# Cross-attention with a gate on one core: running maximum and shift on pairs of score tiles

## The reference

```
memory_proj    = einsum('bme,de->bmd', memory, W_mem)
scores         = einsum('bnd,bmd->bnm', x, memory_proj) / sqrt(512)
attn           = softmax(scores, axis=-1)
memory_context = einsum('bnm,bmd->bnd', attn, memory_proj)
gate  = sigmoid(einsum('bnf,df->bnd', concat[x, memory_context], W_gate) + b_gate)
fused = x + gate * memory_context
out   = fused * rsqrt(mean(fused**2, axis=-1) + 1e-6) * norm_w
```

## Time and profile before

| | us |
|---|---|
| median of 3 runs (lowest, highest) | 561.93 (561.55, 562.57) |
| the profiled execution | 561.31 |
| its span in the trace | 559.5 |
| PE busy | 538.0 |
| DVE busy | 503.5 |
| ACT busy | 335.7 |
| POOL busy | 134.0 |
| one batch of the loop (from 296.17 to 362.19) | 66.02 |

### The profile page before, as it was taken

The page is one execution under the profiler, slowest core; times in us unless marked ns, Lnnn a source line. Parts: engine busy times, 40 slices in busy tenths (PEclk is TensorE's granted clock), DMA queues, the critical chain, the costliest instruction groups (busy, mean ns, idle before and its releaser), DMA issues.

```text
span 559.5 us, 8972 instructions
## 1 busy us (share of the span) xinstructions
PE 538.0 (96%) x2416; PEld 436.4 (78%) x2416; DVE 503.5 (90%) x847; ACT 335.7 (60%) x633; POOL 134.0 (24%) x102
## 2 busy tenths in 40 slices
PE   6999999999999999999999999999999999999992
PEld 5877888878888788878888788887888778887881
DVE  3789859999899998899988998999988999889976
ACT  4666636665567655586366764766556754657534
POOL 0005500244002530055101550024400351005600
PEclk9999999999999999999999999999999999999997
DMA  9974362511684107821276115752078311210033
GB/s 224 261 130 68 95 107 77 100 63 34 141 174 107 37 23 154 170 75 37 89 142 135 56 37 123 164 100 73 0 159 178 85 37 69 69 38 21 0 115 112
DMA packets 184338, 54.25 MB, mean 97 GB/s; under 512 B 161528, under 2 KB 174848, under 8 KB 184320
## 3 DMA queue, kind: packets, MB, share of 16 engines
q1 hardware_dynamic: 183792, 53.52, 41.2%
q10 hardware_dynamic: 528, 0.52, 0.3%
HBM read 45.63 MB, written 8.39 MB: 97 GB/s over the span
## 4 chain that ended last, share of the span: by engine, by line
PE 65%; DVE 19%; issue 10%; ACT 2%; SPq 2%; DMA 1%; ACTq 0%; DVEq 0%
PE bank L355 14%; PE bank L357 13%; PE bank L356 13%; PE bank L516 7%; PE bank L517 7%; PE bank L518 7%; DVE p_lo L830 6%; DVE s L871 3%; DVE fused L976 2%; DVE fused L983 2%; DVE gate L897 2%; ACT fused L688 2%; DVE gate L926 2%; SPq L239 2%; DMA x_raw<-in_x_dram 1%
## 5 line engine op out<-in xcount | busy, mean ns | idle before, releaser
L1147 POOL TENSOR_TENSOR psum_rows<-psum_rows,p_tmp 128x512 f32<-128x512 f32 (+1 forms) x88 | 122.4, 1391 | 86.5 <-ACT p_tmp L665 85.4
L830 DVE TENSOR_TENSOR p_lo<-p_tmp,p_hi 128x512 fp32r<-128x512 f32 (+1 forms) x104 | 92.2, 888 | 4.8 <-ACT p_hi L627 4.8
L665 ACT ACTIVATE p_tmp<-s 128x512 f32<-128x512 f32 (+1 forms) x104 | 65.2, 627 | 45.1 <-DVE s L871 44.4
L1147 POOL TENSOR_TENSOR psum_rows<-p_tmp 128x512 f32<-128x512 f32 x8 | 10.8, 1352 | 309.0 <-ACT p_tmp L665 309.0
L355 PE MATMUL bank<-q_hi,mt_hi 128*128 128x512 f32 (+1 forms) x208 | 81.8, 393 | 0.0
L516 PE MATMUL bank<-p_hi,mem_hi 128*128 128x512 f32 (+1 forms) x208 | 81.2, 390 | 0.1
L356 PE MATMUL bank<-q_lo,mt_hi 128*128 128x512 f32 (+1 forms) x208 | 81.2, 390 | 0.0
L357 PE MATMUL bank<-q_hi,mt_lo 128*128 128x512 f32 (+1 forms) x208 | 81.2, 390 | 0.0
L517 PE MATMUL bank<-p_lo,mem_hi 128*128 128x512 f32 (+1 forms) x208 | 81.1, 390 | 0.0
L518 PE MATMUL bank<-p_hi,mem_lo 128*128 128x512 f32 (+1 forms) x208 | 81.0, 389 | 0.0
L627 ACT ACTIVATE s<-bank 128x512 f32<-128x512 f32 (+1 forms) x104 | 62.0, 596 | 19.4 <-PE bank L357 18.9
(11 more groups left out here) (91 smaller groups left out, 1028.4 us busy)
## 6 DMA issues: line engine op xcount, KB each, us to landing
mem_raw<-in_ctx_dram SPq DMA_DIRECT2D x48, 256.0 KB, 3.0
mem_blocks<-in_ctx_dram SPq DMA_DIRECT2D x64, 136.0 KB
x_again<-in_x_dram SPq DMA_DIRECT2D x32, 256.0 KB, 2.7
out_dram<-fused SPq DMA_DIRECT2D x32, 256.0 KB, 2.1
x_raw<-in_x_dram SPq DMA_DIRECT2D x112, 64.0 KB, 2.1
mem_blocks<-in_ctx_dram SPq DMA_DIRECT2D x56, 64.0 KB, 2.0
x_raw<-in_x_dram SPq DMA_DIRECT2D x4, 256.0 KB, 4.8
gate<-in_L_xattn_W_gate_dram SPq DMA_DIRECT2D x2, 512.0 KB, 5.7
```

The source lines that it names most:

```text
L665: nc.scalar.activation(p_tmp[0:r, t % TMP_RING, :], s[0:r, t, :], ACT.Exp, scale=float(D) ** -0.5).then_inc(exp_done, 1)
L830: return nc.vector.tensor_tensor(dst, src, hi.bitcast(F32), ALU.subtract)
L1147: nc.gpsimd.tensor_tensor(psum_rows[0:r, :], a, p_tmp[0:r, t % TMP_RING, :], ALU.add).then_inc(p_added, 1)
```

## The change

The running maximum and the shift work on two score tiles at a time, 1024 columns in one operation.

- `run` holds two tiles. `running_max(b, p)` takes the pair p (1 to 5) and starts when both tiles of the pair are copied. `fold_max` then takes the maximum of the two halves, and `last_max` takes in tile 12, of 65 rows. That is 7 operations instead of 12.
- `shift(b, p)` subtracts the spread maximum from a pair, with the bank read twice through a broadcast pattern. Tile 12 stays alone. That is 7 operations instead of 13. Two pairs are shifted ahead of the loop over the tiles (before: three tiles), and within it the pair t/2 + 2 at each even t up to 8 (before: tile t + 3 at each t up to 9).
- In the scoring stage the pair's maximum stands behind the low part and the block transpose of its step, and `last_max` stands behind all low parts of the memory. Before, tile 12 was taken in ahead of the low parts 4 and 5.
- The waits on `run_done` and `shifted` count by pairs.

```diff
-            def running_max(b, t):
+            def running_max(b, p):
-                dve.wait_ge(s_copied, MT * b + t + 1)
-                r = rows(t)
-                if t == 1:
-                    a = s[0:r, 0, :]
-                else:
-                    a = run[0:r, :]
-                    dve.wait_ge(run_done, (MT - 1) * b + t - 1)
-                nc.vector.tensor_tensor(run[0:r, :], a, s[0:r, t, :], ALU.max).then_inc(run_done, 1)
+                dve.wait_ge(s_copied, MT * b + 2 * p + 2)
+                if p == 1:
+                    a = s[:, 0:2, :]
+                else:
+                    a = run[:, :, :]
+                    dve.wait_ge(run_done, MP * b + p - 1)
+                nc.vector.tensor_tensor(run[:, :, :], a, s[:, 2 * p : 2 * p + 2, :], ALU.max).then_inc(run_done, 1)
+            def fold_max(b):
+                dve.wait_ge(run_done, MP * b + MP - 2)
+                nc.vector.tensor_tensor(run[:, 0, :], run[:, 0, :], run[:, 1, :], ALU.max).then_inc(run_done, 1)
+            def last_max(b):
+                dve.wait_ge(run_done, MP * b + MP - 1)
+                dve.wait_ge(s_copied, MT * (b + 1))
+                nc.vector.tensor_tensor(run[0:LAST, 0, :], run[0:LAST, 0, :], s[0:LAST, MT - 1, :],
+                                        ALU.max).then_inc(run_done, 1)
...
+                if p < MP - 1:
+                    ts = slice(2 * p, 2 * p + 2)
+                    nc.vector.tensor_tensor(s[:, ts, :], s[:, ts, :],
+                                            bank[MAX_BANK][:, :].rearrange("p (a n) -> p a n", a=1).broadcast_to([P, 2, N]),
+                                            ALU.subtract).then_inc(shifted, 1)
...
             def softmax(b, t, with_x):
-                if t + 3 < MT:
-                    shift(b, t + 3)
+                if t % 2 == 0 and t // 2 + 2 < MP:
+                    shift(b, t // 2 + 2)
...
                 transpose_mem(b, 2)
                 for p in range(MP):
-                    if p >= 1:
-                        running_max(b, 2 * p)
                     if p + 2 < MP:
                         mt_lo_part(b, p + 2)
                     if p + 3 < MP:
                         transpose_mem(b, p + 3)
-                    if 2 * p + 1 < MT:
-                        running_max(b, 2 * p + 1)
+                    if 1 <= p < MP - 1:
+                        running_max(b, p)
+                    if p == MP - 2:
+                        fold_max(b)
                     for q in SPLIT_BY_SCORES.get(p, []):
                         mem_lo_part(b, q)
+                last_max(b)
```

More of the change, by code:

```diff
@@ L113, in xattn_kernel @@
         norm_rows = sb("norm_rows", [P, D])
-        run = sb("run", [P, N])
+        run = sb("run", [P, 2, N])
         psum_rows = sb("psum_rows", [P, N])
@@ L417, in transpose_max @@
             def transpose_max(b):
-                pe.wait_ge(run_done, (MT - 1) * (b + 1))
+                pe.wait_ge(run_done, MP * (b + 1))
                 pe.wait_ge(s_copied, MT * (b + 1))
@@ L424, in transpose_max @@
                     last = nc.tensor.transpose(
-                        bank[S_BANK][:, j * P : (j + 1) * P], run[:, j * P : (j + 1) * P], ident[:, :])
+                        bank[S_BANK][:, j * P : (j + 1) * P], run[:, 0, j * P : (j + 1) * P], ident[:, :])
                 last.then_inc(pe_max_t, 1)
@@ L447, in row_sums @@
                 else:
-                    pe.wait_ge(shifted, MT * (b + 1))
+                    pe.wait_ge(shifted, MP * (b + 1))
                 for j in range(NT):
@@ L654, in exp @@
             def exp(b, t, first):
-                act.wait_ge(shifted, MT * b + t + 1)
+                act.wait_ge(shifted, MP * b + t // 2 + 1)
                 if t >= TMP_RING:
@@ L864, in reduce_max, with shift @@
                                         AX.X, ALU.max).then_inc(col_max_done, 1)
-            def shift(b, t):
-                if t == 0:
+            def shift(b, p):
+                if p == 0:
                     dve.wait_ge(pe_max_rows, b + 1)
-                r = rows(t)
-                nc.vector.tensor_tensor(s[0:r, t, :], s[0:r, t, :], bank[MAX_BANK][0:r, :],
-                                        ALU.subtract).then_inc(shifted, 1)
+                if p < MP - 1:
[4 more added lines that the diff above has]
+                else:
+                    nc.vector.tensor_tensor(s[0:LAST, MT - 1, :], s[0:LAST, MT - 1, :], bank[MAX_BANK][0:LAST, :],
+                                            ALU.subtract).then_inc(shifted, 1)
             def p_lo_part(b, t):
@@ L1046, in iteration @@
                     shift(b, 1)
-                    shift(b, 2)
                     for t in range(MT):
```

## The result

| | before | after |
|---|---|---|
| median of the runs, us | 561.93 (561.55 to 562.57) | 574.89 (574.29 to 575.68) |
| the profiled execution, us | 561.31 | 574.29 |
| its span, us | 559.5 | 572.5 |
| PE busy, us | 538.0 | 537.0 |
| DVE busy, us | 503.5 | 492.8 |

A forecast was written before the change was run, and what follows sets the result against it. PE was taken as the bound, busy 65.15 of 66.02 us per batch. The terms 1.6 - 0.25 + 6 x 1.65 + 1.65 - 0.3 = 12.6 us move the median from 561.93 to 574.5 us; range 568 to 579.5.

The forecast's parts named there:

- The bound: Loop batch: PE busy 65.15 of 66.02 us; less DVE time gives back at most about 1 us per batch.
- The price of a pair: DVE operations on two tiles: engine held 1.13 us, result after 1.21 us; bounds 1.06 and 1.20 us.
- The maximum: End of scoring: last_max starts at 299.13, transposes at 299.88, so PE loses 1.60 us per batch.
- The shifts and add_bias: Shift to weighted 0: add_bias 0 later, one larger wait replaces two at gate_x; weighted 0 late by 1.68 us.
- rival (a): Low part of tile 2 starts before POOL's fourth addition: weighted 0 late by 1.3, not 1.65 us; 572.1 us; 20%.
- The sum: Whole kernel: first batch, six loop batches at 1.65 us and last batch give 12.6 us more, median 574.5.
- (b): First shift depends less on context 0, delay half absorbed at gate_x: 0.85 us lost per batch, 568.7 us; 10%.
- (c): Longer DVE operations let POOL in once more ahead of add_bias 0: about 1 us per batch, 581 us; 10%.
- (d): DVE decides: maximum not late on PE, 0.8 us per batch off the waits at gate_x, 556.3 us; 4%.
- DVE's slack: Past tile 4: DVE has 1.1 us less to do than PE's delay, so xt, q, mt and u come early enough.

The follow-up runs named there:

- e9: Kernel before with the shift on pairs, the maximum on single tiles, and add_bias 0 to 3 moved to t = 2, 3, 5, 6: 551.20 us.
- e12: Kernel before with POOL adding only 64 of the 512 columns: 550.34 us.
- e1: Changed kernel with last_max (tile 12) directly behind the fold, ahead of low parts 3, 4 and 5 of the memory: 577.67 us.
- e6: Changed kernel with the pair shifts in the loop at odd t instead of even t, so six tiles are shifted ahead of add_bias 0: 571.79 us.
- e7: Changed kernel with tiles 0 to 9 as four maximum pairs, tiles 10 to 12 single, pairs shifted at t = 1, 4, 6, 8, 10: 573.56 us.
- e5: Changed kernel with POOL adding only 64 of the 512 columns: 564.45 us.
- e3: Changed kernel with the shift back on single tiles, so only the maximum is on pairs: 575.31 us.
- e8: Kernel before, all on single tiles, with the shifts of tiles 6 to 12 one step later: 563.61 us.
- e10: Kernel before, all on single tiles, with add_bias 0 to 3 moved to t = 2, 3, 5, 6: 564.48 us.
- e11: Four maximum pairs with early fold, tiles 10 to 12 single, pair shifts at even t, add_bias at t = 2, 3, 5, 6; against kernel before: 554.07 us.

## Why the prediction was right

**The bound.** PE was read as the bound, with 0.87 us of idle time per batch. It held: DVE was busy for 10.7 us less and the kernel gained nothing by it. What better timing on DVE can give back was put too low, at about 1 us per batch: e9 and e12 give back 1.5 (66.02 to 64.5), because a stop costs PE its idle time and a slow restart.

**The price of a pair.** Taken as 1.13 us to the next start and 1.21 us in length; the two groups measured 1.208 us (shift) and 1.212 us (maximum):

```profile
L883 DVE TENSOR_TENSOR s<-s,bank 128x1024 f32<-128x1024 f32 x48 | 57.2, 1208 | 0.0
L841 DVE TENSOR_TENSOR run<-run,s 128x1024 f32<-128x1024 f32 x32 | 38.8, 1212 | 7.7 <-ACT s L627 7.7
```

The broadcast bank costs nothing extra. Two shifts in a row take 2.34 us, so the next start comes after 1.13 us, and the fixed part of an operation that reads a bank is 0.07 us (2 x 0.60 less 1.13). The Trainium skill (VectorE: DVE Perf Modes, the section on the TRN2 errata) gives 120 cycles for a PSUM source, which by the prediction's estimate is 0.125 us; here the measurement decides.

**The maximum.** Predicted: last_max from 299.13, transposes from 299.88, late by 1.60 us. Measured in the same frame (minus 6.55): 299.18 and 300.00, late by 1.72 us, of which 1.48 are seen as idle. Of the missing 0.12 us, 0.05 is the later start of last_max, and 0.07 the way from DVE to PE, 0.13 us here and not the 0.06 us taken from add_bias.

**The shifts and add_bias.** gate_input 3 was put at 311.95 and stood at 312.12; the terms given for it (311.35 + 1.6 + 0.5 - 1.4) add up to 312.05, so 0.1 us of the miss is a slip in the sum. From it, POOL's fourth addition was put at +2.70 us and came at +2.70, the low part of tile 2 at +2.85 and came at +2.84, add_bias 0 at +4.5 and came at +4.47. The thin margin of rival (a), 0.15 us, fell as forecast, to POOL, by 0.14 us; that is right but partly luck, since other times of the stepping are off by as much. gate_x 3 no longer waits, and weighted 0 starts at 322.89 in this frame (329.44), 1.77 us late where 1.68 were forecast.

**The sum.** Forecast 12.6 us, measured 12.96 (574.89 - 561.93). By parts, from the starts of the transposes in batches 1 and 7: up to batch 1 forecast 2.95, measured 3.14 (100.24 to 103.38), the excess being in the first transposes, which were 1.85 us late (38.01 to 39.86) and not 1.6; six batches of the loop forecast 9.9, measured 10.1 (396.14 to 406.24); the rest forecast -0.25, measured -0.3 (from 63.14 to 62.87 us).

**What the prediction had not seen.** It presented the 1.60 us as the price of the maximum alone. e1 shows that it is the larger of two lags at the end of scoring: with the order of the last maximum put right, DVE is still behind with the pair, the fold and the low parts, and PE waits for add_bias 0 instead. It also read DVE's slack as safe up to the end of the batch; that held for the change, but e6 and e7, which shift later, used it up at mt_lo. The rivals (b), (c) and (d) did not occur; the waits that (b) relied on were POOL's, as e5 and e12 show.

## What to carry to other kernels

Merging operations saves a fixed part each, but makes the first result of the merged work later and lets it start only when the last of its inputs is there; where the merged work ends a stage that another engine waits for, take the last pieces one by one, and put nothing ahead of them that this engine does not need. Follow the engine that had its order changed to the end of the period, and not just to the next wait. Where a two-operand operation can be held by another engine's access, place the results that the bounding engine waits for ahead of the operations that are held.

## What the runs showed of the hardware that was not expected

- TensorE's granted clock fell to 1.2 GHz for some 3 us behind a wait of 2.16 us in e1. It did not fall in the changed kernel behind waits of 1.48 and 1.21 us in the same batch, nor in three of the seven batches of e1, behind waits of 2.13 to 2.15 us, such as the one from 101.07 to 168.32 us; the four with a fall had 2.05 to 2.16 us.
- The length of the wait ahead does not decide it alone, and what else does is not shown. In the last batch the clock also fell in e3, e8, e10 and e11, behind waits for u_lo of 0.4, 0.6, 2.0 and 0.6 us, and not in the kernel before behind one of 0.3 us. In e8 (stretches as above):

```profile
539.30:542.70 3.40, 3.40 (x9) 2.63 (x8) 0.99 (x3) 0.63 (x1) 0.00 (x0) 0.50 0.66 203
```

- Additions on POOL held DVE for so long that the kernel before is 11.6 us (2%) faster with short ones (e12), though POOL is busy for 24% of the span only.
- A stop of PE costs more than its idle time: in e6, 0.12 us of idle time cost 0.4 us.
